# Block boundary reordered in a fused cross-attention and FFN kernel: an earlier scale broadcast, a value projection ahead of the second row tile, one broadcast a step later

## The reference, cut to what matters

```python
def layer(x, ctx, mask, w_q, w_k, w_v, w_out, w12, b12, w3, b3):     # x, ctx: 16 sequences x 128 rows x 1024
    q, k, v = layernorm(x) @ w_q.T, ctx @ w_k.T, ctx @ w_v.T         # 32 query heads, 8 key/value groups, 32 wide
    p = softmax(where(mask, q_h @ k_g.T / sqrt(32), lowest))         # per sequence, head h of group g
    x = x + concat(p @ v_g) @ w_out.T
    x12 = layernorm(x) @ w12.T + b12                                 # 2048 wide
    x1, x2 = split(x12, 2)
    return x + (silu(x1) * x2) @ w3.T + b3
```

## Time and profile before

| | |
|---|---|
| median of 3 runs | 1057.46 us |
| lowest, highest | 1057.0, 1063.34 us |
| the profiled execution, its time | 1063.34 us |
| its span in the profile | 1061.4 us |
| TensorE busy | 1028.9 us, 97% of the span |
| VectorE busy | 683.5 us, 64% |
| ScalarE busy | 429.2 us, 40% |
| GpSimd busy | 492.9 us, 46% |

### The profile page before, as it was taken

The page is one execution under the profiler, slowest core; times in us unless marked ns, Lnnn a source line. Parts: engine busy times, 40 slices in busy tenths (PEclk is TensorE's granted clock), DMA queues, the critical chain, the costliest instruction groups (busy, mean ns, idle before and its releaser), DMA issues.

```text
span 1061.4 us, 21836 instructions
## 1 busy us (share of the span) xinstructions
PE 1028.9 (97%) x8400; PEld 701.2 (66%) x8400; DVE 683.5 (64%) x2092; ACT 429.2 (40%) x967; POOL 492.9 (46%) x456
## 2 busy tenths in 40 slices
PE   8897899999999999999899999999999999999998
PEld 7776767867778677786655544444444888468853
DVE  6789978777787776687846432836865346625431
ACT  5766545645546455565475320113431112301110
POOL 2769811634626345267887689138842301212000
PEclk8999899999999999999999999999999999999999
DMA  9659597999999887599784634395759641884201
GB/s 366 222 145 194 133 276 174 236 222 209 255 205 239 217 222 195 133 227 235 178 225 111 174 144 172 86 306 210 247 182 219 246 120 41 212 243 122 81 30 50
DMA packets 230775, 199.11 MB, mean 188 GB/s; under 512 B 177040, under 2 KB 187280, under 8 KB 225808
## 3 DMA queue, kind: packets, MB, share of 16 engines
q1 hardware_dynamic: 230672, 197.72, 68.4%
HBM read 119.04 MB, written 35.65 MB: 146 GB/s over the span
## 4 chain that ended last, share of the span: by engine, by line
PE 79%; DVE 10%; DMA 3%; POOL 2%; issue 1%; SPq 0%; ACT 0%; DVEq 0%; POOLq 0%; ACTq 0%
PE bank_dense L1322 47%; PE bank_spare L1322 11%; PE bank_score L1467 6%; PE bank_spare L1467 5%; DVE arena_attn L1790 3%; PE bank_av L1467 3%; PE bank_score L1379 2%; DMA arena_attn<-arena_attn 2%; DVE arena_in L1629 1%; DVE arena_attn L1800 1%; PE bank_av L1397 1%; PE bank_av L1401 1%; PE bank_av L1399 1%; DMA arena_rows<-w_t 1%; DVE arena_rows L1684 1%
## 5 line engine op out<-in xcount | busy, mean ns | idle before, releaser
L1137 ACT ACTIVATE arena_attn<-arena_attn,arena_in 128x128 f32<-128x128 f32 x512 | 162.7, 391 | 121.1 <-DVE arena_in L1790 120.9
L920 POOL TENSOR_TENSOR arena_attn<-arena_attn 128x512 f16<-128x512 f32 x85 | 99.0, 1181 | 156.7 <-ACT arena_attn L1144 156.7
L1322 PE MATMUL bank_dense<-arena_rows,arena_in 128*128 128x256 f16 (+1 forms) x1200 | 167.4, 297 | 1.6 <-POOL arena_in L865 1.0
L1322 PE MATMUL bank_dense<-arena_attn,arena_rows 128*128 128x512 f16 x768 | 166.4, 379 | 0.0
L1322 PEld LDWEIGHTS bank_dense<-arena_rows,arena_in 128*128 128x128 f16 x1200 | 116.3, 98 | 42.2 <-DVE arena_in L1641 1.3
L1790 DVE CUSTOM_DVE_ANT_0 arena_attn<-bank_score,arena_in 128x128 f32<-128x128 f32 x512 | 143.5, 345 | 0.4 <-POOL arena_attn L920 0.3
L1322 PEld LDWEIGHTS bank_dense<-arena_attn,arena_rows 128*128 128x128 f16 x768 | 75.2, 98 | 90.2
L1322 PE MATMUL bank_dense<-arena_out,arena_attn 128*128 128x512 f16 x552 | 123.8, 382 | 0.0
L1322 PE MATMUL bank_spare<-arena_rows,arena_in 128*128 128x256 f16 (+1 forms) x720 | 96.0, 290 | 0.0
L1322 PEld LDWEIGHTS bank_dense<-arena_out,arena_attn 128*128 128x128 f16 x552 | 53.6, 99 | 61.8 <-issue 1.8
L1322 PEld LDWEIGHTS bank_spare<-arena_rows,arena_in 128*128 128x128 f16 x720 | 70.0, 98 | 19.7
(11 more groups left out here) (217 smaller groups left out, 1880.9 us busy)
## 6 DMA issues: line engine op xcount, KB each, us to landing
arena_rows<-x SPq DMA_DIRECT2D x32, 512.0 KB, 5.8
arena_in<-w_scratch SPq DMA_DIRECT2D x64, 256.0 KB, 3.0
arena_attn<-q_scratch SPq DMA_DIRECT2D x48, 256.0 KB, 4.3
arena_rows<-w_t SPq DMA_DIRECT2D x12, 1024.0 KB, 6.3
arena_rows<-ctx_t SPq DMA_DIRECT2D x8, 1024.0 KB, 5.9
q_scratch<-arena_attn SPq DMA_DIRECT2D x16, 512.0 KB, 5.3
x_scratch<-arena_rows SPq DMA_DIRECT2D x16, 512.0 KB, 4.0
arena_out<-x_scratch SPq DMA_DIRECT2D x16, 512.0 KB, 6.0
```

Of the source, the lines that this page charges most:

```text
L920: ins = pool.tensor_tensor(p_split[:, g % 2, u, 1], e[:, g % 2, u], p_split[:, g % 2, u, 0], ALU.subtract)
L1137: ins = act.activation(head, head, ACT.Exp, bias=neg_max[:, g % 2, h:h + 1], scale=-1.0)
L1322: ins = pe.matmul(dst, lhs(a, c), rhs(b, c), start=(c == chunks[0] and n == 0), stop=(c == chunks[-1] and n == 2))
```

## The change

Three edits, each made in `dense_order()` and in the programs of the engines concerned:

1. The output weights' scale `"o"` is made in step `(1, 1)` and no longer in `(1, 0)`.
2. In steps 1 and 7 (`SPREAD_EARLY`) `spread_top` stands right behind the first unit and the first row tile, ahead of `turn_attn`, and `take_top` on VectorE ahead of `attn_lo`. That concerns `"o"` in `(1, 1)` and `ctx2` to `ctx7` in `(1, 7)` to `(6, 7)`. Other scales stay at the step's end.
3. The second unit goes ahead of the second row tile on TensorE, ScalarE and VectorE. That concerns `v(t,1)` and tile `2t+3` in step 7 of blocks 1 to 7, and `k(7,0)` and tile 17 in `(7, 3)`.

GpSimd's and SyncE's programs keep their order. The core of the diff:

```diff
+SPREAD_EARLY = (1, 7)
 def top_at(t, s):
-    if t == 1 and s == 0:
+    if t == 1 and s == 1:
         return "o"
...
                     if tile is not None:
                         turn_x(tile, 0)
                         turn_x(tile, 1)
+                    if name and s in SPREAD_EARLY:
+                        spread_top(name)
                     if t == NB and s in H_AT:
                         hidden(0, H_AT[s], 0)
                     if g >= 3:
                         turn_attn(g - 3)
+                    unit(second_unit(t, s))
                     if tile2 is not None:
                         turn_x(tile2, 0)
                         turn_x(tile2, 1)
-                    unit(second_unit(t, s))
                     if t == NB and s in H_AT:
                         hidden(0, H_AT[s], 1)
-                    if name:
+                    if name and s not in SPREAD_EARLY:
                         spread_top(name)
...
                     exps(g, 1)
+                    unit_hi(second_unit(t, s))
                     if tile2 is not None:
                         x_hi(tile2, 0)
                         x_hi(tile2, 1)
-                    unit_hi(second_unit(t, s))
...
                     if tile is not None:
                         x_lo(tile, 0)
                         x_lo(tile, 1)
+                    if name and s in SPREAD_EARLY:
+                        take_top(name)
...
+                    unit_lo(second_unit(t, s))
                     if tile2 is not None:
                         x_lo(tile2, 0)
                         x_lo(tile2, 1)
-                    unit_lo(second_unit(t, s))
                     if t == NB and s in H_AT:
                         gate(0, H_AT[s])
-                    if name:
+                    if name and s not in SPREAD_EARLY:
                         take_top(name)
```

More of the change, by code:

```diff
@@ L187, in dense_order @@
                 n += [("x", tile, 0), ("x", tile, 1)]
+            if name and s in SPREAD_EARLY:
+                n.append(("spread", name))
             if t == NB and s in H_AT:
@@ L191, in dense_order @@
                 n.append(("a", g - 3))
+            if second_unit(t, s):
+                n.append(second_unit(t, s))
             if tile2 is not None:
                 n += [("x", tile2, 0), ("x", tile2, 1)]
-            if second_unit(t, s):
-                n.append(second_unit(t, s))
             if t == NB and s in H_AT:
                 n.append(("h", 0, H_AT[s], 1))
-            if name:
+            if name and s not in SPREAD_EARLY:
                 n.append(("spread", name))
```

## The result

| | before | after |
|---|---|---|
| median | 1057.46 us | 1067.28 us (1065.51 to 1073.94) |
| ratio after to before | | 1.0078, 95% interval 1.0053 to 1.0102 |
| span of the profiled execution | 1061.4 us | 1063.3 us |
| TensorE busy in it | 1028.9 us | 1024.2 us |
| VectorE busy in it | 683.5 us | 685.4 us |

The changed kernel is slower by 0.8%, some 8 to 10 us. That is inside the 1% that the prediction calls "same", and the interval leaves no doubt of the sign. The forecast was +4.1 us: the direction was right, the size half of what came. By the ratio the changed kernel stands at 1065.7 us, inside the range from 1054 to 1067, but above the band from 1059 to 1063 that the forecast itself claimed; it lies between the bands of two rivals whose mechanism, the clock, didn't come.

A forecast was written before the change was run, and what follows sets the result against it. TensorE's program was taken as the path almost everywhere, with 11.4 us of waits aimed at. 1.2 + 1.4 + 0.9 + 3.0 - 2.4 = +4.1 us on the median 1057.46 gave 1061.6 us, range 1054 to 1067.

The forecast's parts named there:

- The wait moves to the broadcast: Expected in the changed kernel's waits: L1315 on L1602 about 7 times, over 6 us; `v_low` wait only in block 7.
- Steps (1,0) and (1,1): Block 1: the spread starts after 2.7 us of idle TensorE, `scores(2)` comes at 75.5 instead of 73.98, +1.5 us.
- so the loss is carried on: Block 1 after step (1,1): VectorE has nearly no gap, so the +1.5 us stays, less 0.3: +1.2, lower end 0.
- The clock, +1.4: Step (1,1): the new 2.7 us of idle time lowers TensorE's clock for the projection behind it, +1.4 us.
- Block 1's step 7, +0.9: The spread waits until 113.4, `v1` starts 0.7 earlier, the tile's tail costs more: +0.9 us, between 0 and 1.5.
- Blocks 2 to 6, +3.0: Step 7: the next block's first projection waits for the second row tile's low half, 5 x 0.6 = +3.0 us.
- Block 7, -2.4: Step 7: `v1` fills the 3.03 us wait, `hidden(0,0,0)` starts at 524.05 instead of 526.46: -2.4 us, bounds 0 and -3.5.
- VectorE's `mask_scores` of step 0 starts 0.6 later with it, but the next scores have 2 us of room: Behind the boundaries of blocks 2 to 6: masked scores come 0.6 us later, with 2 us of room before the next scores.
- The tail is hidden: Rival: the second tile's low half comes in time, `v1` fills the old wait: -1.7 us, 1052.5 to 1055.8; chance 0.2.
- Nothing measurable: Rival: block 1's losses vanish in its transfers, blocks 2 to 6 cancel with block 7: about 1058 us; chance 0.2.
- The clock falls at the boundaries: Rival: two waits within 5 us in each of blocks 2 to 6 cause half rate: +11.6 us, 1069; chance 0.05.
- Block 3 and one other: Rival: the clock falls at only these boundaries, +1.6 to +3.2 us more, 1063.2 to 1064.8; chance 0.15.

The follow-up runs named there:

- before, run again: The kernel before, unchanged, run once more for a second profile: 0.9996 (0.9977 to 1.0015), span 1056.0 us.
- the two versions that keep the swap: Kernel before with edit 3 and `output_scales` moved to step 2: 0.9966; the same with `"o"` in step (1,1), no early broadcast: 0.9960.

## Why the prediction was right or wrong, step by step

- **The wait moves to the broadcast: right.** Forecast over 6 us in about 7 places; 10.2 us in 6 places came, 4.5 of it in block 1. The row tile's wait for `v_low` stayed only in block 7, with 0.9 us.
- **Steps (1,0) and (1,1): right in place, too dear in total.** The wait was forecast at 2.7 us and was 2.27; scores(0) to scores(2) took 14.84 us, 1.53 more than the 13.31 of the profile that the prediction read (forecast 1.5) and 2.02 more than in before, run again. But the step "so the loss is carried on", with +1.2, isn't borne out: block 1 as a whole lost 0.6, less than it varies by, and the run with these edits alone measured +0.7 us (1.0007), which can't be told from nothing.
- **The clock, +1.4: wrong.** After 2.27 us of idle time the next 24 matmuls took 2.79 us. Three projections took over 4 us, as in the profile that the prediction read. The longest stands in step 7 of block 1, where the prediction had no term for the clock: `v(1,1)` took 4.57 us. TensorE there, in the changed kernel and then in before, run again:

```profile
113.04 0.58 PE L1320 MATMUL bank_spare<-small,arena_in 1*128 1x2 f32 x2 [4.53 <-DVE small L1609]
...
114.51 4.57 PE L1327 MATMUL bank_dense<-arena_in 128*128 128x256 f16 x24 [0.27 <-DVE v_low L1766]
```

```profile
111.02 0.63 PE L1346 MATMUL bank_spare<-arena_in,arena_rows 128*128 128x128 f32 x4 [1.32 <-DVE small L1611]
113.59 1.12 PE L1346 MATMUL bank_spare<-arena_in,arena_rows 128*128 128x128 f32 x4 [1.94 <-DVE v_low L1779]
114.50 3.87 PE L1337 MATMUL bank_dense<-arena_in 128*128 128x256 f16 x24
```

- **Block 1's step 7, +0.9: the mis-sized term.** It measured +2.4. In before two waits, 1.32 and 1.94 us, have a row tile's half between them; after, everything stands behind one of 4.53 and one of 0.27 us: 4.80 against 3.26 us, +1.5. `v(1,1)` at the lower clock is another +0.7. The prediction had the place of both waits right (spread at 113.4, forecast from the earlier trace rows, here 113.04) but took `v1` to start 0.7 us earlier than the tile's half did, and at an unchanged clock. With the edits of block 1's first steps alone, boundary 1 already takes 22.87 us, 1.3 more than in before, without an edit in it, and so does the kernel with the swap in block 7 alone, 22.97 us, in which no edit stands before block 7. There the waits were 2.01 and 1.94 us and `v(1,1)` took 5.26 us instead of 3.87. So up to 1.4 us of the 2.4 can come without the edits, through the clock; how much did isn't settled.
- **Blocks 2 to 6, +3.0: right.** The five boundaries lost 0.56, 0.81, 0.80, 0.69 and 0.67 us, 3.5 in all, and the new wait on the row tile's low half is in the table with 3.1 us in six places, 0.5 at most. The 0.6 us that were forecast for each were good to 0.1 on average.
- **Block 7, -2.4: right in number, partly by luck.** It measured -2.3 against before, again. `v(7,1)` filled the wait, and 1.26 us of idle time stand in front of `hidden(0,0,0)` (528.35), which needs the low half of the last row tile (VectorE ends it at 528.25): the tail, as worked out. But 1.7 of the 2.3 us are the clock: `v(7,1)` took 2.78 us instead of 4.46. In the kernel with the early broadcast alone, where nothing in block 7 is edited, the wait was 2.21 us and not 3.02, `v(7,1)` kept the higher clock, and the boundary took 22.42 us, less than the 23.03 of the changed kernel. The kernel before with `output_scales` moved shows the same (2.15 us, 22.37). So the edit gains here only where the longer wait comes. TensorE in before, run again, then with the early broadcast alone:

```profile
515.09 0.66 PE L1346 MATMUL bank_spare<-arena_in,arena_rows 128*128 128x128 f32 x4 [3.02 <-DVE v_low L1779]
515.69 4.46 PE L1337 MATMUL bank_spare<-arena_in 128*128 128x256 f16 x24
```

```profile
519.28 0.66 PE L1346 MATMUL bank_spare<-arena_in,arena_rows 128*128 128x128 f32 x4 [2.21 <-DVE v_low L1779]
519.88 2.79 PE L1337 MATMUL bank_spare<-arena_in 128*128 128x256 f16 x24
```

- **"VectorE's `mask_scores` of step 0 starts 0.6 later with it, but the next scores have 2 us of room": the step that failed.** It left out the small operation that stands in front of the masked scores. The later row tile pushed it behind the start of GpSimd's, which made it 0.8 us longer, and the masked scores of block 3 came 1.8 us later and not 0.6. That reached TensorE through a queue that I had not followed: +1.7 us in steps 1 to 3 of block 3, which the moved operation takes back (1.64), and about 5 us in the time, of which the profiles don't place the rest. The prediction followed the order of instructions on VectorE and the room behind, and took durations as fixed.
- **The sum.** Forecast +4.1 = 1.2 + 1.4 + 0.9 + 3.0 - 2.4. By the timelines it was 0.6 + 0 + 2.4 + 3.5 - 2.0 (both rows of block 7) + 3.1 = +7.6. The 3.1 stand in steps 1 to 3 of blocks 2 and 3: 1.7 in block 3, the collision's, and 1.4 in block 2, of unknown cause. Of the 3.5 us that were missing, 3.1 are these, 1.5 the boundary of block 1, 0.5 the tails and 0.4 block 7, less 2.0 of block 1. The two misses in block 1 nearly cancelled, which is luck; what made the forecast too small are the steps behind the heads of blocks 2 and 3, which had no term in it. This is an account of one profile against one: against the profile that the prediction read, the same pipeline is longer by 3.2 us and not by 7.8. Only the loss at boundaries 2 to 6, that in block 3 and the measured ratios stand above this scatter.
- **The rivals.** "The tail is hidden" fell: waits of 0.42 to 0.53 us stand in the trace at all five boundaries. "Nothing measurable" fell by the ratio's interval. "The clock falls at the boundaries", of which the rule of the Trainium skill (TensorE: Matmul & The Clock Gate, Part 1: The HAM clock gate) was the ground, didn't come where it was looked at: 24 matmuls took 2.78 us between the waits of 0.70 and 0.53 us at the boundary of block 4, and 2.79 us behind them. "Block 3 and one other" is nearest in number, but block 3 shows no fall of the clock either: the granted clock was 1.00 from 245 to 262 us, and its boundary took 16.98 us, 0.81 more than before, like the others.

What stays open: how much the second collision costs the two versions that keep the swap, how boundary 1 splits, why block 2 varies, and why the wait of boundary 7 is 2.2 us in some kernels and 3.0 in others that do the same work there.

## What to carry to other kernels

A wait that an engine can't avoid belongs where unrelated work still follows it: putting `v(t,1)` into the old wait gained at boundaries 1 to 5, while pulling the broadcast forward lost, since it stands in front of everything and waits for the end of a chain, not for its start. When an edit shifts an engine by half a microsecond, ask of its short operations whether they now start beside another engine's longer one, and move those that nobody waits for. A change that gains where it was aimed and not in the time has given it back elsewhere, and a table of the times of all steps finds the place, if a second profile of the unchanged kernel says which rows of it repeat.

## What the runs showed of the hardware

- A VectorE operation on 128x4 numbers took 0.23 us when it started 0.19 us ahead of GpSimd's 1.16 us operation, and 1.00 to 1.06 us when it started just behind it; then both ended together. Another on 128x512 numbers took 0.67 to 0.81 us in the other kernels and 1.68 us when it started 0.02 us behind an operation of GpSimd of 1.15 us.
- TensorE kept its clock over an idle gap of 2.27 us (24 matmuls of 2.79 us behind it), over one of 2.21 us (2.79) and over 0.70 us (2.78). Behind 3.02 us the same 24 took 4.46 us, behind 4.53 us 4.57 us, behind 1.32 and 1.94 us close together 3.87 us, and behind 2.01 and 1.94 us 5.26 us. In the changed kernel 24 matmuls also took 4.45 us behind a gap of only 1.81 us in block 1, so the length of the last gap alone doesn't tell.
- A DMA transpose of probabilities in block 3 took 8.2 us from issue to landing in before, run again, and 9.2 us in the changed kernel.
